# Handing the expert weights to the DMA queue one pair of rows later in a fused MoE, attention, MoE layer

## The chip, the cores and the metric

The kernel runs on one core of a Trainium2 chip. The metric is the device time of one execution in microseconds (us); a version is judged by the median of several executions.

## What is computed

The input `x` is 2048 tokens (4 sequences of 512) of 512 numbers in float32. The layer adds three terms to it, one after the other:

```
x = x + 0.5 * moe(layernorm(x))
x = x + attention(layernorm(x))        # 32 heads, causal, ALiBi, q and k layer-normed
x = x + 0.5 * moe(layernorm(x))        # same weights as the first

def moe(x):
    logits = x @ W_gate + b_gate                       # 8 experts
    top2   = the two experts with the largest logits
    y_all  = relu(x @ W_e[e] + b_e[e])                 # for each expert e, 512 x 512 weights
    return mean of the two chosen y_all
```

## The kernel before, in words

The program is a row of blocks: routing 1, experts 1, qkv, attention, routing 2, experts 2. The change lies in `route_block`, which is called for both routings.

**What a routing block does.** The 2048 tokens are taken as 8 *pairs* of row tiles; pair `u` holds tiles `2u` and `2u+1` of 128 tokens each. For each pair the block loads the rows (`load_x`), computes the layer norm on VectorE (DVE), ending in two `TENSOR_SCALAR` instructions that write `xn` (line 1289), stores the plain rows into the accumulator (`store_x`, line 1021) and the normalised rows into DRAM for the later gather (`store_xn`, line 1025). TensorE (PE) transposes the normalised rows (`transpose`, four matmuls per tile by line 1121), ScalarE (ACT) copies the transpose out of PSUM (`copy`, line 1209), and PE multiplies it with the gate weights (`gate`, line 1144). When the gates of all 16 tiles are there, DVE starts the choice of the experts at line 1298 (`route_logits`), a long chain which ends in the tables that the expert block reads.

**The expert weights.** Beside this the block brings the 8 MB of expert weights in, as 16 *pieces* of 512 KB, two per expert. Piece `n` is loaded into `w_lo` (`load_weights`, line 1031), ACT rounds it into `w_hi` (`weights(n)`, line 1213), and GpSimd (POOL) takes the difference back into `w_lo` (line 1109). No piece is used before the expert block.

**Routing 2 has more to do per pair.** There the attention's output projection is done on the way (`proj`): `load_o` brings in a tile of attention output (line 1017), PE transposes it (`o_transpose`), ACT splits it (`o_split`, line 1204), DVE takes the rest (`o_rest`, line 1251), PE multiplies (`out_proj`, twelve matmuls per tile, lines 144 to 146), and DVE adds the result to the row (`add_x`, line 1257) before its layer norm.

**What sets the order.** Every engine runs its own instruction list in the order in which it is written, and waits on semaphores. All the loads and stores named here are issued by SyncE (SP) from one list. ACT's list for pair `u` of routing 2 is: `o_split(2u+2)`, `weights(2u)`, `o_split(2u+3)`, `copy` of the two tiles of pair `u-1`, `weights(2u+1)`; in routing 1 it is the same without the `o_split`. DVE's list for pair `u` of routing 2 is: `add_x(2u)`, `o_rest(2u+2)`, statistics, `add_x(2u+1)`, `o_rest(2u+3)`, statistics, the reciprocal root, the two writes of `xn`. PE's list for pair `u` is: the gates of pair `u-2`, `out_proj(2u)`, `o_transpose(2u+2)`, `out_proj(2u+1)`, `o_transpose(2u+3)`, the transposes of pair `u-1`.

On SP, `store_xn(u)` waits until the `xn` of pair `u` is written, and all that is written behind it in SP's list waits with it. `load_x(u)` waits for its buffer from pair 4 on.

Of the kernel before, what the change touches and what calls it, by code (L numbers as in the profile page):

```python
# [900 lines left out]
def route_block(nc, prefix, ex, x_in, xn_dram, acc, w_gate, b_gate, w_e, b_e, o_dram=None, wo_turned=None, w_qkv=None, w_turned=None):  # L901
# [4 lines left out]
    with ExitStack() as ctx:  # L906
# [93 lines left out]
        PAIRS = TILES // 2  # L1000


        def pair_rows(dram, u):
            return dram[2 * P * u:2 * P * (u + 1), :].rearrange("(p k) d -> p k d", k=2)

        @block.sync
        def _(sp):
            def load_x(u):
                if u >= XR:
                    sp.wait_ge(xn_done, 2 * (u - XR) + 2)  # L1010
                    sp.wait_ge(x_stored[u % XR], 16 * (u // XR))
                sp.dma_start(x[u % XR][:, :, :], pair_rows(x_in, u)).then_inc(x_loaded[u % XR], 16)

            def load_o(t):
                if t >= 2:
                    sp.wait_ge(o_tr, t - 1)
                sp.dma_start(o[t % 2][:, :], pair_rows(o_dram, t // 2)[:, t % 2, :]).then_inc(o_loaded[t % 2], 16)

            def store_x(u):
                sp.wait_ge(sum_done if proj else x_loaded[u % XR], 2 * u + 2 if proj else 16 * (u // XR + 1))  # L1020
                sp.dma_start(pair_rows(acc, u), x[u % XR][:, :, :]).then_inc(x_stored[u % XR], 16)

            def store_xn(u):
                sp.wait_ge(xn_done, 2 * u + 2)
                sp.dma_start(pair_rows(xn_dram, u), xn[u % 2][:, :, :]).then_inc(xn_stored[u % 2], 16)

            def load_weights(n):

                if n >= WR:
                    sp.wait_ge(w_hi_done, n - WR + 1)  # L1030
                sp.dma_start(ex.w_lo[:, 2 * n:2 * n + 2, :].bitcast(F32), w_e[n // 2, :, :].rearrange("(p c) h -> p c h", c=C)
                             [:, 2 * (n % 2):2 * (n % 2) + 2, :]).then_inc(w_loaded[n % WR], 16)

            if proj:
                load_o(0)
                load_o(1)
            load_x(0)
            sp.dma_start(g_raw[:, :, :], w_gate.rearrange("(c p) e -> p c e", p=P)).then_inc(g_loaded, 16)
            sp.dma_start(bg_bc[:, :], b_gate.rearrange("(a e) -> a e", a=1).to_broadcast([P, E])).then_inc(bias_loaded, 16)
            if proj:  # L1040
                load_o(2)
                load_o(3)
            load_x(1)
            load_weights(0)
            load_weights(1)
            for u in range(PAIRS):
                if u + 2 < PAIRS:
                    load_x(u + 2)
                if u >= 1:
                    store_xn(u - 1)  # L1050
                if u + 1 < PAIRS:
                    load_weights(2 * u + 2)
                    load_weights(2 * u + 3)
                if proj and 2 * u + 4 < TILES:
                    load_o(2 * u + 4)
                    load_o(2 * u + 5)
                store_x(u)

            def load_wq(n):
                if n < 2:  # L1060

                    sp.wait_ge(xn_done, 2 * (n + XR) + 2)
                    sp.wait_ge(x_stored[n], 16 * (PAIRS // XR))
                else:
                    sp.wait_ge(wq_tr, 2 * n - 2)
                sp.dma_start(w_stage[n % 2][:, :, :], w_qkv[2 * P * n:2 * P * (n + 1), :].rearrange("(k p) d -> p k d", p=P)
                             ).then_inc(wq_loaded[n % 2], 16)

            if w_qkv is not None:
                load_wq(0)  # L1070
                load_wq(1)
            store_xn(PAIRS - 1)
            if w_qkv is not None:
                for n in range(2, WQ_PAIRS):
                    load_wq(n)
                sp.wait_ge(wq_tr, 2 * WQ_PAIRS)
            for i in range(XR):
                sp.wait_ge(x_stored[i], 16 * (PAIRS // XR))
            sp.wait_ge(xn_done, TILES)
            sp.dma_start(ex.bias[:, :], b_e.rearrange("(a e) h -> a (e h)", a=1).to_broadcast([P, E * D])).then_inc(ex.bias_loaded, 16)  # L1080
            sp.wait_ge(bias_loaded, 16)
            for par in range(2):
                sp.wait_ge(xn_stored[par], 16 * (PAIRS // 2))
# [488 lines left out]
```

## Time and profile before

| | |
|---|---|
| median of 3 executions | 1024.22 us (1021.04 to 1028.01) |
| the profiled execution | 1027.31 us, its span 1025.6 us |
| routing 1, from the start to the first expert gather | 92.8 us |
| routing 2, from the end of attention to the first expert gather | 747 to 873 us of the span |
| PE busy | 873.8 us, 85% of the span |
| DVE busy | 638.0 us, 62% |
| ACT busy | 444.2 us, 43% |
| POOL busy | 353.1 us, 34% |

Times in rows of the trace are counted from the start of the span. The profiled execution is 3.1 us above the median and within the range of the three. A bracket at the end of a row of the timeline gives the idle time of the engine before it, and what ended it.

### The profile page before, as it was taken

How to read it: one execution, taken by the hardware profiler on the slowest of the kernel's cores; microseconds unless marked ns; L12 is line 12 of the kernel's file. 1: busy time of each engine (PE TensorE's matmuls, PEld its weight loads, DVE VectorE, ACT ScalarE, POOL GpSimd, SP SyncE). 2: the span in 40 equal slices, each digit the busy share in tenths (PEclk: the TensorE clock that was granted, in tenths of full speed). 3: DMA queues.
4: the chain of work that ended last, by engine and by line, in shares of the span. 5: the costliest groups of instructions: out<-in, count | busy, mean ns of one | idle time of the engine just before them, and what ended most of it. 6: DMA issues, size and time to landing. Idle time of an engine off the chain costs nothing. (4 is left out here: it accounts for less than half of the span.)

```text
span 1025.6 us, 20208 instructions
## 1 busy us (share of the span) xinstructions
PE 873.8 (85%) x6688; PEld 646.5 (63%) x6689; DVE 638.0 (62%) x1296; ACT 444.2 (43%) x818; POOL 353.1 (34%) x342
## 2 busy tenths in 40 slices
PE   4874999992999989769999999999859993799994
PEld 4773888871777767645555555555447872688883
DVE  7955344433988877757777777777246768244441
ACT  3431333332244434527767677777623430233331
POOL 6723677763123222300000000000034420677764
PEclk9995999996999999959999999999979975799997
DMA  9954588762165599464666666562078850477863
GB/s 339 373 194 170 106 149 149 144 120 71 42 194 171 173 222 232 154 178 115 159 136 135 134 131 137 137 147 75 23 237 300 314 196 31 109 145 145 149 130 51
DMA packets 112859, 162.08 MB, mean 158 GB/s; under 512 B 16864, under 2 KB 74336, under 8 KB 112512
## 3 DMA queue, kind: packets, MB, share of 16 engines
q1 hardware_dynamic: 94928, 123.85, 41.5%
q0 software_dynamic: 17856, 37.25, 19.1%
q8 instruction: 45, 0.74, 0.3%
q14 instruction: 30, 0.25, 0.1%
HBM read 97.44 MB, written 67.37 MB: 161 GB/s over the span
## 5 line engine op out<-in xcount | busy, mean ns | idle before, releaser
L829 DVE TENSOR_REDUCE att_part<-att_s_ps 128x2 f32<-128x1024 f32 (+2 forms) x160 | 195.5, 1225 | 60.9 <-PE att_s_ps L677 60.5
L791 ACT ACTIVATE att_prob<-att_st_ps 128x512 f32<-128x512 f32 x320 | 173.7, 595 | 78.7 <-PE att_st_ps L703 78.6
L144 PE MATMUL exp_z_ps<-ex_w_hi,exp_xT_hi 128*128 x312 | 132.1, 423 | 1.3 <-DVE exp_xT_lo L1482 0.7
L146 PE MATMUL exp_z_ps<-ex_w_hi,exp_xT_lo 128*128 x312 | 126.2, 404 | 0.0
L145 PE MATMUL exp_z_ps<-ex_w_lo,exp_xT_hi 128*128 x312 | 125.8, 403 | 0.0
L1482 DVE TENSOR_TENSOR exp_xT_lo<-exp_t_ps,exp_xT_hi 128x512 fp32r<-128x512 f32 x78 | 54.0, 692 | 107.2 <-ACT exp_xT_hi L1468 107.2
L1475 ACT ACTIVATE exp_y<-exp_y 128x512 f32<-128x512 f32 x72 | 45.5, 632 | 168.7 <-DVE exp_y L1494 168.7
L1109 POOL TENSOR_TENSOR ex_w_lo<-ex_w_lo,ex_w_hi 128x1024 fp32r<-128x1024 f32 x32 | 76.2, 2395 | 96.2 <-ACT ex_w_hi L1213 64.9
L716 PE MATMUL att_pv_ps<-att_prob,att_v_sb 128*32 128x256 f32 (+2 forms) x1280 | 101.4, 391 | 1.8 <-ACT att_oT L796 1.8
L1410 POOL DMA_INDIRECT exp_xg<-xn,ex_token_of x78 | 78.1, 1002 | 66.2 <-SPq L1382 38.7
L641 POOL CAST att_m_parts<-att_part 128x28 fp32r<-128x28 f32 x32 | 6.6, 208 | 270.3 <-DVE att_part L833 270.3
L1494 DVE TENSOR_TENSOR exp_y<-exp_z_ps,ex_bias 128x512 f32<-128x512 f32 x72 | 49.8, 692 | 67.0 <-PE exp_z_ps L146 66.4
L144 PE MATMUL qkv_o_ps<-qkv_w_hi,qkv_xT_hi 128*128 128x512 f32 x192 | 81.8, 426 | 1.9 <-DVE qkv_xT_lo L436 1.6
L146 PE MATMUL qkv_o_ps<-qkv_w_hi,qkv_xT_lo 128*128 128x512 f32 x192 | 77.5, 404 | 0.0
L145 PE MATMUL qkv_o_ps<-qkv_w_lo,qkv_xT_hi 128*128 128x512 f32 x192 | 77.5, 403 | 0.0
L1434 POOL DMA_INDIRECT out<-exp_y,ex_row_of x39 | 62.1, 1591 | 27.4 <-DMA out<-exp_y,ex_row_of 12.3
L144 PEld LDWEIGHTS exp_z_ps<-ex_w_hi,exp_xT_hi 128*128 128x128 f32 x312 | 61.3, 197 | 14.2 <-issue 2.7
L1448 PE MATMUL exp_t_ps<-exp_ident,exp_xg 128*128 128x128 f32 x312 | 51.4, 290 | 21.3 <-DMA exp_xg<-xn,ex_token_of 21.3
L146 PEld LDWEIGHTS exp_z_ps<-ex_w_hi,exp_xT_lo 128*128 128x128 f32 x312 | 60.2, 193 | 14.2
L1448 PEld LDWEIGHTS exp_t_ps<-exp_ident,exp_xg 128*128 128x128 f32 x312 | 50.2, 206 | 29.6 <-issue 17.2
L145 PEld LDWEIGHTS exp_z_ps<-ex_w_lo,exp_xT_hi 128*128 128x128 f32 x312 | 60.4, 194 | 11.3
L656 PE MATMUL att_s_ps<-st_masks 64*128 64x256 bf16 (+1 forms) x640 | 57.7, 260 | 10.4 <-PEq L211 7.8
(199 smaller groups left out, 1644.0 us busy)
## 6 DMA issues: line engine op xcount, KB each, us to landing
ex_w_lo<-in_L_ffn_W_e SPq DMA_DIRECT2D x32, 512.0 KB, 5.7
v_vals<-st_vals SPq DMA_DIRECT2D x16, 512.0 KB, 2.8
q_parts<-st_partq SPq DMA_DIRECT2D x32, 256.0 KB, 3.4
k_parts<-st_partk SPq DMA_DIRECT2D x32, 256.0 KB, 3.7
att_v_sb<-v_vals SPq DMA_DIRECT2D x32, 256.0 KB, 3.7
ex_bias<-in_L_attn_hidden_states SPq DMA_DIRECT2D x8, 512.0 KB, 7.8
acc<-ex_bias SPq DMA_DIRECT2D x8, 512.0 KB, 8.6
xn<-route_xn SPq DMA_DIRECT2D x8, 512.0 KB, 5.5
```

What stands on the lines that cost most here:

```text
L144: nc.tensor.matmul(out, x_hi[:, s], w_hi(c), start=(c == 0), stop=False)
L145: nc.tensor.matmul(out, x_hi[:, s], w_lo(c), start=False, stop=False)
L146: last = nc.tensor.matmul(out, x_lo[:, s], w_hi(c), start=False, stop=(c == C - 1))
L656: nc.tensor.matmul(blocks_of(banks[half], where), mine[:, 0, :], rhs, start=(c == 0), stop=False, skip_group_check=True)
L716: last = nc.tensor.matmul(pv_ps[VW * h:VW * (h + 1), j * P + c0:j * P + c1], v_sb[n % RING][:, j, VW * h:VW * (h + 1)], prob[n % 2][:, col ...
L791: nc.scalar.activation(prob[n % 2][:, col:col + 512], st_ps[(e + half) % 3][:, :], ACT.Exp).then_inc(exp_done, 1)
L829: nc.vector.tensor_reduce(out, src, X_AXIS, ALU.max, negate=True).then_inc(red_done, 1)
L1109: nc.gpsimd.tensor_tensor(ex.w_lo[:, 2 * n:2 * n + 2, :], ex.w_lo[:, 2 * n:2 * n + 2, :].bitcast(F32), ex.w_hi[:, 2 * n:2 * n + 2, :].bitc ...
L1410: nc.gpsimd.indirect_dma_start(out=xg[s % RING][:, :], out_offset=None, in_=xn_dram[:, :], in_offset=bass.IndirectOffsetOnAxis(ap=ex.token ...
L1434: nc.gpsimd.indirect_dma_start(out=acc[:, :], out_offset=bass.IndirectOffsetOnAxis(ap=ex.row_of[:, s:s + 1], axis=0), in_=y[s % RING], in_ ...
L1448: last = nc.tensor.transpose(t_ps[r % 2][:, c * P:(c + 1) * P], xg[r][:, c:D:C], ident[:, :])
L1482: nc.vector.tensor_tensor(xT_lo[r % 2][:, :], t_ps[r % 2][:, :], xT_hi[r % 2][:, :].bitcast(F32), ALU.subtract).then_inc(lo_done, 1)
```

## The change

Before, pieces 0 and 1 are issued ahead of the loop, and the turn of pair `u` issues the pieces `2u+2` and `2u+3`. Now the turn of pair `u` issues the pieces `2u` and `2u+1`, from `u = 1` on. The turn of pair 0 issues none, and the turn of pair 7, which issued none before, issues pieces 14 and 15. Nothing is added or taken away: the same 16 transfers stand one turn later in SP's list.

```
                 if u >= 1:
                     store_xn(u - 1)
-                if u + 1 < PAIRS:
-                    load_weights(2 * u + 2)
-                    load_weights(2 * u + 3)
+                if u >= 1:
+
+                    load_weights(2 * u)
+                    load_weights(2 * u + 1)
                 if proj and 2 * u + 4 < TILES:
```

The lists of ACT, DVE, PE and POOL keep their order. SP's list of routing 2 from the load of pair 1's rows on, before (`ex_bias<-acc` is `load_x`, `ex_w_lo` a pair of pieces, `route_o` the attention output, `out` `store_x`, `xn` `store_xn`):

```order
L1012 DMA ex_bias<-acc 128x1024
L1031 DMA ex_w_lo<-in_L_ffn_W_e 128x1024 x2
L1012 DMA ex_bias<-acc 128x1024
L1031 DMA ex_w_lo<-in_L_ffn_W_e 128x1024 x2
L1017 DMA route_o<-o_vals 128x512 x2
L1021 DMA out<-ex_bias 128x1024
L1012 DMA ex_bias<-acc 128x1024
L1025 DMA xn<-wo_turned 128x1024
L1031 DMA ex_w_lo<-in_L_ffn_W_e 128x1024 x2
```

And the same place in the changed program:

```order
L1012 DMA ex_bias<-acc 128x1024
L1031 DMA ex_w_lo<-in_L_ffn_W_e 128x1024 x2
L1012 DMA ex_bias<-acc 128x1024
L1017 DMA route_o<-o_vals 128x512 x2
L1021 DMA out<-ex_bias 128x1024
L1012 DMA ex_bias<-acc 128x1024
L1025 DMA xn<-wo_turned 128x1024
L1031 DMA ex_w_lo<-in_L_ffn_W_e 128x1024 x2
```

The pair of pieces that stood ahead of pair 0's stores has gone; pieces 2 and 3 now stand behind the store of pair 0's `xn`, where 4 and 5 stood.

SP's list at the end of routing 1, before, from the store of pair 4's `xn` on (`acc<-ex_bias` is `store_x` here, `in_L_attn_Wqkv` the load of the attention weights):

```order
L1025 DMA xn<-route_xn 128x1024
L1031 DMA ex_w_lo<-in_L_ffn_W_e 128x1024 x2
L1021 DMA acc<-ex_bias 128x1024
L1025 DMA xn<-route_xn 128x1024
L1031 DMA ex_w_lo<-in_L_ffn_W_e 128x1024 x2
L1021 DMA acc<-ex_bias 128x1024
L1025 DMA xn<-route_xn 128x1024
L1021 DMA acc<-ex_bias 128x1024
L1066 DMA ex_bias<-in_L_attn_Wqkv 128x2x512 x2
```

And the changed program, from the same store on:

```order
L1025 DMA xn<-route_xn 128x1024
L1031 DMA ex_w_lo<-in_L_ffn_W_e 128x1024 x2
L1021 DMA acc<-ex_bias 128x1024
L1025 DMA xn<-route_xn 128x1024
L1031 DMA ex_w_lo<-in_L_ffn_W_e 128x1024 x2
L1021 DMA acc<-ex_bias 128x1024
L1025 DMA xn<-route_xn 128x1024
L1031 DMA ex_w_lo<-in_L_ffn_W_e 128x1024 x2
L1021 DMA acc<-ex_bias 128x1024
```

The last pair of pieces, 14 and 15, now stands behind the store of pair 6's `xn`; it stood behind that of pair 5.

## Rows read from the trace of the kernel before

**Rows 1.** Busy time by stretch: window, length, engines, PE clock, DMA share, GB/s
```profile
9.00:29.00 20.00, 14.05 (x61) 12.47 (x62) 18.69 (x45) 10.74 (x14) 16.03 (x7) 1.00 1.02 419
46.00:54.00 8.00, 6.52 (x29) 5.63 (x28) 7.45 (x20) 2.98 (x4) 5.11 (x3) 1.00 0.87 265
771.00:775.00 4.00, 4.00 (x12) 3.09 (x11) 1.29 (x2) 1.40 (x2) 2.38 (x1) 0.59 0.94 281
780.00:790.00 10.00, 9.70 (x59) 8.23 (x59) 7.59 (x23) 4.06 (x6) 5.14 (x3) 1.00 0.89 316
```
**Rows 2.** ACT's waits for the pieces, routing 1 (total us, times, longest)
```profile
ACT ex_w_hi L1213 <- DMA ex_w_lo<-in_L_ffn_W_e: 32.5, 9, 8.0
```
**Rows 3.** ACT's waits for the pieces, routing 2
```profile
ACT ex_w_hi L1213 <- DMA ex_w_lo<-in_L_ffn_W_e: 1.2, 1, 1.2
```
**Rows 4.** Timeline of SP, routing 2: start, us, queue, line, transfer
```profile
781.39 0.32 SPq L1025 DMA_DIRECT2D xn<-wo_turned  x1
...
791.40 0.65 SPq L1031 DMA_DIRECT2D ex_w_lo<-in_L_ffn_W_e  x1
```
**Rows 5.** DMA issues of 781.3 to 782: last figure us from issue to landing
```profile
xn<-wo_turned SPq DMA_DIRECT2D x1, 512.0 KB, 3.0
ex_w_lo<-in_L_ffn_W_e SPq DMA_DIRECT2D x1, 512.0 KB, 4.9
```
**Rows 6.** DMA issues of 791 to 791.6, the next pair's first piece
```profile
ex_w_lo<-in_L_ffn_W_e SPq DMA_DIRECT2D x1, 512.0 KB, 5.2
```
**Rows 7.** Timeline of ACT, routing 2, turn of pair 2
```profile
782.56 1.05 ACT L1213 ACTIVATE ex_w_hi<-ex_w_lo 128x1024 fp32r<-128x1024 f32 x1
785.28 0.60 ACT L1204 ACTIVATE route_oT_hi<-route_o_ps 128x512 fp32r<-128x512 f32 x1 [1.67 <-PE route_o_ps L1121]
785.77 1.08 ACT L1209 ACTIVATE route_xT<-route_t_ps 128x512 f32<-128x512 f32 x2
```
**Rows 8.** Timeline of DVE, routing 2
```profile
769.28 1.00 DVE L1289 TENSOR_SCALAR wo_turned<-ex_bias,route_mv,route_rstd 128x512 f32<-128x512 f32 x2
...
785.91 0.69 DVE L1251 TENSOR_TENSOR route_oT_lo<-route_o_ps,route_oT_hi 128x512 fp32r<-128x512 f32 x1 [0.30 <-ACT route_oT_hi L1204]
...
789.86 1.15 DVE L1289 TENSOR_SCALAR wo_turned<-ex_bias,route_mv,route_rstd 128x512 f32<-128x512 f32 x2
...
830.01 3.19 DVE L1289 TENSOR_SCALAR wo_turned<-ex_bias,route_mv,route_rstd 128x512 f32<-128x512 f32 x2
...
846.00 0.29 DVE L1298 TENSOR_TENSOR route_logits<-route_g_ps,route_bg_bc 128x128 f32<-128x128 f32 x1 [5.12 <-PE route_g_ps L1144]
```
**Rows 9.** Timeline of PE, routing 2
```profile
770.16 0.66 PE L1121 MATMUL route_o_ps<-route_ident,route_o 128*128 128x128 f32 x4 [2.72 <-DMA route_o<-o_vals]
...
786.41 1.95 PE L1144 MATMUL route_g_ps<-route_g_raw,route_xT 128*128 128x8 f32 x16 [0.30 <-ACT route_xT L1209]
...
840.48 1.97 PE L1121 MATMUL route_t_ps<-route_ident,wo_turned 128*128 128x128 f32 x8 [1.71 <-DVE wo_turned L1289]
842.28 3.59 PE L1144 MATMUL route_g_ps<-route_g_raw,route_xT 128*128 128x8 f32 x16
```
**Rows 10.** Timeline of ACT, routing 1: piece 14
```profile
54.97 1.06 ACT L1213 ACTIVATE ex_w_hi<-ex_w_lo 128x1024 fp32r<-128x1024 f32 x1 [5.34 <-DMA ex_w_lo<-in_L_ffn_W_e]
```
**Rows 11.** Timeline of PE, routing 1: gates of pair 6, transposes of pair 7
```profile
56.56 3.58 PE L1144 MATMUL route_g_ps<-route_g_raw,route_xT 128*128 128x8 f32 x16 [1.81 <-ACT route_xT L1209]
59.99 1.95 PE L1121 MATMUL route_t_ps<-route_ident,route_xn 128*128 128x128 f32 x8
```
**Rows 12.** Timeline of DVE, routing 1: `xn` of pair 7, start of the choice
```profile
57.17 2.02 DVE L1289 TENSOR_SCALAR route_xn<-ex_bias,route_mv,route_rstd 128x512 f32<-128x512 f32 x2
65.49 0.29 DVE L1298 TENSOR_TENSOR route_logits<-route_g_ps,route_bg_bc 128x128 f32<-128x128 f32 x1 [6.30 <-PE route_g_ps L1144]
```
**Rows 13.** Instructions of line 1289, routing 1: ns min/median/max
```profile
L1289 DVE TENSOR_SCALAR route_xn<-ex_bias,route_mv,route_rstd x16: 534/1394/2652, 8.5 to 58.7; 128x512 f32<-128x512 f32 x16
```
**Rows 14.** Instructions of line 1109, routing 1: ns min/median/max
```profile
L1109 POOL TENSOR_TENSOR ex_w_lo<-ex_w_lo,ex_w_hi x16: 2338/2358/2540, 11.3 to 71.1; 128x1024 fp32r<-128x1024 f32 x16
```

## The prediction

> **What bounds the kernel now.** The change touches only the two routing blocks, so I read those two stretches, first by busy time, then by waits, then instruction by instruction at the last pair. What is to be found is the thing that DVE's choice of experts waits for, since all that follows hangs on it.
>
> Routing 1 is bound by its transfers. From 9 to 29 us the DMA engines are full at 419 GB/s [rows 1], so one transfer of 512 KB (524,288 bytes) takes 1.25 us of the queue, and ACT waits nine times, 32.5 us in all, for a piece to land [rows 2]. These waits matter, because ACT's list puts `weights(2u)` ahead of the copies of pair u-1. The end shows it: piece 14 releases ACT at 54.97, the copies of pair 6 follow [rows 10], PE gates pair 6 from 56.56, released by them, and transposes pair 7 from 59.99 without a wait [rows 11]; its gates end the block, and the choice starts at 65.49 [rows 12]. From the landing of piece 14 to the choice there are 10.5 us of unbroken chain. A second path ends at the same point: the `xn` of pair 7 is written at 57.17 + 2.02 = 59.19 [rows 12].
>
> Routing 2 is bound by PE: 9.70 of 10 us busy at the full clock between 780 and 790 [rows 1], and ACT waits for a piece once, 1.2 us, in the whole block [rows 3]. The pieces are there ahead of their use, because they were issued a turn earlier. Piece 4, which ACT takes at 782.56 [rows 7], stood behind the store of pair 0's `xn`, written at 769.28 + 1.00 = 770.28 [rows 8], and so was issued some 12 us before its use.
>
> **The change, routing 2.** Call X(u) the time at which the `xn` of pair u is written. After the change, pieces 2u and 2u+1 are issued behind the store of X(u-1) and wanted by ACT within turn u. Behind `weights(2u)` in ACT's list stand `o_split(2u+3)` and the copies of pair u-1. DVE's `o_rest(2u+3)` waits for that split, and X(u) comes behind it in DVE's list. So a loop of one pair closes, which was two pairs long before: X(u-1), issue, landing, `weights`, `o_split`, `o_rest`, X(u). Its length from rows:
> - X to the issue of the first piece: the write of pair 2 ends at 789.86 + 1.15 = 791.01 [rows 8], the piece is issued at 791.40 [rows 4]: 0.39 us.
> - Issue to landing behind the `xn` store on a short queue: 4.9 and 5.2 us [rows 5, 6]; I take 5.05. The neighbours in SP's list are the same as before, so the queue in front should be too.
> - `weights(2u)` on ACT: 1.05 us [rows 7].
> - Start of the split to start of the rest: 785.91 - 785.28 = 0.63 us [rows 7, 8].
> - `o_rest` to X: 791.01 - 785.91 = 5.10 us [rows 8].
>
> That makes 12.2 us. Turns 1 to 6 have the split, so six of them lie between X(0), which the change does not move (770.28), and X(6): 770.3 + 73.3 = 843.6. Before, X(6) was 830.01 + 3.19 = 833.20 [rows 8], so this is 10.4 us later.
>
> What was late before is covered then: PE needs some 9.65 us per pair (X(2) at 791.01 against X(1), which released the store at 781.39 [rows 4]) and will wait some 2.5 us in each. The row loads and `route_o` loads that now go ahead of pieces 2 and 3 do arrive sooner, but nothing is won by it, because X(1) waits for piece 2.
>
> The tail: `weights(14)` stands ahead of the copies of pair 6, so after X(6) come 0.39 + 5.05 + 1.05, then 0.64 from the copies to the gates (785.77 to 786.41 [rows 7, 9]), the gates of pair 6, and from the transposes of pair 7 to the choice 846.00 - 840.48 = 5.52 [rows 8, 9]. The gates took 1.95 us at 786, in the stretch of full clock, and 3.59 at 842 [rows 1, 9]. PE will have waited there, so both are possible: 14.6 or 16.2 us, against 846.00 - 833.20 = 12.8 before. The middle is 2.6 more. Routing 2: **+13.0 us**.
>
> The least is set by the landing: a store behind an empty queue lands in 3.0 us [rows 5], plus one transfer of 1.25 us makes 4.25 and a loop of 11.4, so +8. The most: a piece behind a longer queue. In routing 1 the pace of five transfers per pair is 6.25 us; with that as the landing time the loop is 13.4 and the block +20.
>
> The Trainium skill bears on the landing. "DMA: Bandwidth & Descriptors", section "Rules for kernel authors", says to issue a DMA early and wait for it late, so that its fixed cost overlaps with compute; that rule speaks against this change. The same page, section "Anatomy of one DMA — SWDGE (gpsimd) path", fits some 2.0 us plus the bytes at 436 GB/s, for transfers that GpSimd issues; an estimate from it for a store and a piece of 512 KB is 4.4 us, a loop of 11.6 and a block of +9. The rows above show 4.9 and 5.2 on SP's queue, and I keep to them.
>
> **The change, routing 1.** No `o_split` stands here, but the copies still stand behind `weights(2u)`. In SP's list piece 14 had 34 transfers of 512 KB ahead of it (8 row loads, 6 `acc` and 6 `xn` stores, 14 pieces); now it has 36, one `acc` and one `xn` store more. On a full queue that is 2 x 1.25 = 2.5 us, and the chain of 10.5 us behind piece 14 carries it to the choice. It need not be all: between 46 and 54 the queue moved only 265 GB/s [rows 1], and where the queue has run empty, a store ahead of the piece costs less. Against it stands a gain on the other path: the last `xn` should come earlier, since its rows go ahead and fewer pieces lie on POOL in its way (below). But that path only ended level with the pieces' path, so its gain is not seen. I take **+2.0 us**, from -1 (the queue's slow stretch does not come again) to +4 (it comes, and the store of pair 6 is late).
>
> **The sum.** 13.0 + 2.0 = 15 us. The profiled execution, 1027.3 us with 1.7 us outside its span, would become 1042.3; the median of the three runs is 3.1 us below it, so I predict 1024.2 + 15 = **1039 us**. The experts, qkv and attention carry the shift without a change: no piece is wanted there before all are long done.
>
> **The rivals.**
> - *Rows first pays: faster.* In routing 1 the two `xn` writes take 0.53 us alone, but 1.39 in the median and up to 2.65 [rows 13], while POOL works on a piece for 2.36 us [rows 14]: 16 x (1.39 - 0.53) is some 14 us in which pieces hold up rows. Each pair then has its pieces behind it and not beside it. If the writes were the only path, the last pair would be ready about two piece times earlier, 4 to 5 us, and with routing 2 still fed in time the kernel would take 1020 us. It decides at ACT: for a choice 4 us earlier piece 14 must land by 51 us, where it landed at 55 with two transfers less ahead of it, and for routing 2 to keep its old mean of 62.9 / 6 = 10.5 us per pair a piece must land 3.3 us after its issue. The nine waits [rows 2] and the 4.9 us [rows 5] speak against it. The Trainium skill, "SBUF — State Buffer", section "SBUF: two separate sides", says that VectorE and GpSimd share a port pair as an exclusive lock for a whole instruction; by that rule such writes wait for the rest of a piece, and the kernel with the lock out of the way is this rival's 1020. The trace agrees with the lock (2.65 against 0.53 us). I give it 5%.
> - *The loop is looser than I count.* With the least landing, 4.25 us, routing 2 loses 8 us, and with the better end of routing 1 the sum is +7: 1031, within 1%. For it speaks that the queue in routing 2 is shorter when one pair's rows no longer share a turn with PE's full pace; against it, that the store and the two pieces were alone behind one row load in [rows 5, 6] already. 13%.
> - *PE falls to the low clock and becomes the bound.* Behind a wait of 2.72 us [rows 9] PE's granted clock was 0.59 of full from 771 to 775 [rows 1], so mostly the lower level, 1.2 GHz in place of 2.4. In the loop it waits 2.5 us per pair. A short fall fits into that wait. If the clock stays low for a whole pair, 9.65 us of PE work become 19.3, 7 us beyond the loop; in two of the six pairs that is +14: 1053. 10%.
>
> **How the numbers follow.** The forecast has 72%, the rivals 5, 13 and 10. Its own ends are +8 - 1 and +20 + 4; ends of both at once are unlikely, so I take it from 1030 to 1048, which holds the looser loop too; the faster rival, the PE rival and a few outliers lie outside, under 2 in 10. A measurement of this kernel tells about 1%, 10 us, from no change. Slower by more than that means above 1034.5: most of the forecast and all of the PE rival, 0.79. Within 1%: the looser loop, the rows-first case in part and the lowest of the forecast, 0.18. Faster: 0.03.
>
> **What would show it.** Right: in routing 2, ACT waits for pieces in turns 1 to 7 where it waited once, the writes of `xn` stand 12.2 us apart, each piece is issued 0.4 us behind a write, PE is idle some 2 us per pair, and the choice starts near 859. In routing 1 the copies of pair 6 still stand right behind a wait for piece 14, and the choice starts at 66 to 68. Wrong: the writes of `xn` stay about 10 us apart, or PE waits for nothing in routing 2; or routing 1 ends by more than 2 us earlier.

## The result, and the profile after

The changed kernel takes **1046.87 us** (median of 4 executions, 1044.92 to 1052.87) against 1026.12 us for the kernel before (4 executions, the three shown above and one more beside it). The ratio is 1.0202, with a 95% interval of 1.0164 to 1.024: 17 to 25 us slower. The forecast was +15 us and 1039 us, in a range of 1030 to 1048: right in direction, and in range near its upper end, but 5 to 6 us too small. The profiled execution took 1046.21 us, its span 1044.5 us, 18.9 us more than the span before. The lines from 1052 on stand one number higher than before; each later version is quoted by the line numbers of its own kernel.

In **routing 2** ACT now waits for pieces, and PE for ACT. The waits of the two engines, 745 to 865 us (total us, times, longest):

```profile
ACT ex_w_hi L1214 <- DMA ex_w_lo<-in_L_ffn_W_e: 30.2, 7, 10.2
...
PE route_g_ps L1145 <- ACT route_xT L1210: 17.3, 7, 6.3
```

Before, ACT waited once, 1.2 us [rows 3], and PE's waits at the same place were short:

```profile
PE route_g_ps L1144 <- ACT route_xT L1209: 2.1, 7, 0.3
```

The loop can be read off one turn, that of pair 4. SP's timeline:

```profile
810.31 0.32 SPq L1025 DMA_DIRECT2D xn<-wo_turned  x1
810.67 1.27 SPq L1031 DMA_DIRECT2D ex_w_lo<-in_L_ffn_W_e  x2
...
822.58 0.32 SPq L1025 DMA_DIRECT2D xn<-wo_turned  x1
```

Its first piece in the DMA issues of 810.5 to 811 (last figure, us from issue to landing):

```profile
ex_w_lo<-in_L_ffn_W_e SPq DMA_DIRECT2D x1, 512.0 KB, 5.2
```

ACT's timeline of the same turn:

```profile
810.99 0.60 ACT L1205 ACTIVATE route_oT_hi<-route_o_ps 128x512 fp32r<-128x512 f32 x1 [3.92 <-PE route_o_ps L1122]
815.91 1.06 ACT L1214 ACTIVATE ex_w_hi<-ex_w_lo 128x1024 fp32r<-128x1024 f32 x1 [4.31 <-DMA ex_w_lo<-in_L_ffn_W_e]
816.87 0.58 ACT L1205 ACTIVATE route_oT_hi<-route_o_ps 128x512 fp32r<-128x512 f32 x1
```

And DVE's:

```profile
809.13 1.15 DVE L1290 TENSOR_SCALAR wo_turned<-ex_bias,route_mv,route_rstd 128x512 f32<-128x512 f32 x2
...
817.48 0.69 DVE L1252 TENSOR_TENSOR route_oT_lo<-route_o_ps,route_oT_hi 128x512 fp32r<-128x512 f32 x1 [2.95 <-ACT route_oT_hi L1205]
...
821.43 1.12 DVE L1290 TENSOR_SCALAR wo_turned<-ex_bias,route_mv,route_rstd 128x512 f32<-128x512 f32 x2
```

The write of `xn` ends at 810.28, the piece is issued at 810.67 and rounded from 815.91, the split follows at 816.87, the rest at 817.48, and the next write ends at 822.55: 12.27 us around, where the forecast had 12.2. ACT stood 4.31 us in front of the piece, with the split that DVE wanted behind it.

Not every turn is that clean. In the turn of pair 2 the split was released by PE and not by the piece, as ACT's timeline shows, and the stretch 783 to 788 by busy time (columns as in [rows 1]) shows why:

```profile
789.27 1.05 ACT L1214 ACTIVATE ex_w_hi<-ex_w_lo 128x1024 fp32r<-128x1024 f32 x1
791.99 0.60 ACT L1205 ACTIVATE route_oT_hi<-route_o_ps 128x512 fp32r<-128x512 f32 x1 [1.67 <-PE route_o_ps L1122]
```
```profile
783.00:788.00 5.00, 5.00 (x14) 3.78 (x13) 0.58 (x2) 0.00 (x0) 0.00 (x0) 0.50 0.68 199
```

PE had waited 6.3 us in the turn before and came back at the low level of its clock (granted 0.50, 1.2 GHz). It started 14 matmuls in those 5 us and was late for the split, which began 1.67 us behind the rounding that it would otherwise have followed at once. That turn took 14.1 us.

The tail, on DVE and on PE (two timelines):

```profile
846.21 1.15 DVE L1290 TENSOR_SCALAR wo_turned<-ex_bias,route_mv,route_rstd 128x512 f32<-128x512 f32 x2
...
864.92 0.29 DVE L1299 TENSOR_TENSOR route_logits<-route_g_ps,route_bg_bc 128x128 f32<-128x128 f32 x1 [9.43 <-PE route_g_ps L1145]
```
```profile
855.99 3.58 PE L1145 MATMUL route_g_ps<-route_g_raw,route_xT 128*128 128x8 f32 x16 [4.81 <-ACT route_xT L1210]
859.42 1.95 PE L1122 MATMUL route_t_ps<-route_ident,wo_turned 128*128 128x128 f32 x8
```

X(6) is 847.36, and the choice starts 17.6 us later (12.8 before [rows 8]). Piece 14 took 6.6 us to land (DMA issues of 847.6 to 848), and the gates of pair 6 took the slow 3.58 us, at a granted clock of 0.50 from 856.00 to 859.40:

```profile
ex_w_lo<-in_L_ffn_W_e SPq DMA_DIRECT2D x1, 512.0 KB, 6.6
```

The choice had been forecast near 859. From its first transfer (747.07 before, 748.17 now) to the choice, routing 2 takes 116.8 us in place of 98.9: **+17.8 us**.

In **routing 1** the chain behind piece 14 is the same, later. ACT, PE and DVE:

```profile
57.75 1.06 ACT L1214 ACTIVATE ex_w_hi<-ex_w_lo 128x1024 fp32r<-128x1024 f32 x1 [4.15 <-DMA ex_w_lo<-in_L_ffn_W_e]
```
```profile
59.35 3.58 PE L1145 MATMUL route_g_ps<-route_g_raw,route_xT 128*128 128x8 f32 x16 [1.74 <-ACT route_xT L1210]
62.78 1.95 PE L1122 MATMUL route_t_ps<-route_ident,route_xn 128*128 128x128 f32 x8
```
```profile
53.78 3.12 DVE L1290 TENSOR_SCALAR route_xn<-ex_bias,route_mv,route_rstd 128x512 f32<-128x512 f32 x2
...
68.28 0.29 DVE L1299 TENSOR_TENSOR route_logits<-route_g_ps,route_bg_bc 128x128 f32<-128x128 f32 x1 [11.39 <-PE route_g_ps L1145]
```

Piece 14 lands 2.8 us later than before [rows 10], and the choice starts 2.8 us later [rows 12], a little behind the 66 to 68 of the forecast. The rows did go ahead: the last `xn` is written at 56.90 in place of 59.19. But PE takes it up at 62.78 only, so that gain buys nothing. The shift of 2.8 us does not reach routing 2 whole: in this pair of traces the first gather of experts 1 comes 2.4 us later (92.81 and 95.16), and routing 2 starts 1.1 us later.

### The profile page after: what moved, and what is told of

Its sections match the earlier page's. It is cut to its first block and busy times, and to the rows that moved or that the text cites. A ratio compares the mean times of both kernels' runs of the same rounds, so it can differ in the third digit from the quotient of the medians.

```text
span 1044.5 us, 20208 instructions
## 1 busy us (share of the span) xinstructions
PE 874.2 (84%) x6688; PEld 648.2 (62%) x6689; DVE 632.9 (61%) x1296; ACT 444.1 (43%) x818; POOL 352.1 (34%) x342
## 5 line engine op out<-in xcount | busy, mean ns | idle before, releaser
L1145 PE MATMUL route_g_ps<-route_g_raw,route_xT 128*128 128x8 f32 x256 | 49.7, 331 | 33.4 <-ACT route_xT L1210 33.4
L1145 PEld LDWEIGHTS route_g_ps<-route_g_raw,route_xT 128*128 128x128 f32 x256 | 48.2, 289 | 38.3 <-ACT route_xT L1210 38.3
L1435 POOL DMA_INDIRECT out<-exp_y,ex_row_of x39 | 62.1, 1591 | 27.4 <-issue 12.2
L1449 PEld LDWEIGHTS exp_t_ps<-exp_ident,exp_xg 128*128 128x128 f32 x312 | 50.4, 206 | 30.8 <-issue 17.6
```

Source lines behind the costliest of these rows:

```text
L1145: last = nc.tensor.matmul(g_ps[:, t * E:(t + 1) * E], xT[t % 2][:, c * P:(c + 1) * P], g_raw[:, c, :], start=(c == 0), stop=(c == C - 1))
L1435: nc.gpsimd.indirect_dma_start(out=acc[:, :], out_offset=bass.IndirectOffsetOnAxis(ap=ex.row_of[:, s:s + 1], axis=0), in_=y[s % RING], in_ ...
L1449: last = nc.tensor.transpose(t_ps[r % 2][:, c * P:(c + 1) * P], xg[r][:, c:D:C], ident[:, :])
```

## The experiments

The theory is the loop: a piece issued behind the store of pair u-1, rounded by ACT in turn u ahead of what DVE needs for pair u. Its rivals: the pieces cost by their place in the queue or on POOL beside the writes of `xn` (queue and port), or by what PE's clock does after a wait. Each ratio is against the kernel before on the same chip, which took 1028.05, 1024.06 or 1026.06 us there. The us given with a ratio are worked out from it; the difference of the two medians deviates from them by up to 1.3 us.

**One block at a time.** In `route_block`, the new condition for one of the two blocks and the old one for the other (in the second run with `if proj`):

```
-                if u + 1 < PAIRS:
-                    load_weights(2 * u + 2)
-                    load_weights(2 * u + 3)
+                if not proj:
+                    if u >= 1:
+                        load_weights(2 * u)
+                        load_weights(2 * u + 1)
+                elif u + 1 < PAIRS:
+                    load_weights(2 * u + 2)
+                    load_weights(2 * u + 3)
```

Routing 1 alone. 

> Pieces later in routing 1 alone. Loop theory (a piece wanted by ACT in the turn in which it is issued; its price in routing 1 is two transfers in front of piece 14, since ACT copies pair 6 behind it): choice of experts of routing 1 starts 2 to 3 us later (67.5 to 68.5), the whole +2 to +3 us, 1028 to 1029. Rows-first rival: 3 to 4 us faster. If the blocks did not add up (a shift of routing 1 being lost in qkv and attention): 0 to +1.

Measured: 1031.76 against 1028.05 us, ratio 1.0036 (1.0010 to 1.0062): +3.7 us, slightly more than expected. The choice of this trace stands at 71.16 us, later than in the whole change (68.28) with the same code up to there, so single traces of this block differ by some 3 us. Without the change in routing 1 it stands at 65.49, 64.64 and 64.02 in three traces (the kernel before, routing 2 alone, the half dose below), so both traces with the change are later than all three.

Routing 2 alone. 

> Pieces later in routing 2 alone. Loop theory: X(0) unmoved, then some 12.5 us between the writes of xn, +17 to +18 us in the block, 1043 us in all, ACT waiting some 30 us for pieces. Clock theory gives the same sum here. Rows-first rival: not above 1030.

Measured: 1047.6 against 1028.05 us, ratio 1.0178 (1.0126 to 1.0229): +18.3 us, as the loop theory expected. ACT waits 29.0 us for pieces, and routing 2 takes 113.8 us to its choice. The two parts add up to the whole within their intervals.

**The loop cut at ACT.** In the changed program:

```
                 if proj and u + 1 < PAIRS:
                     o_split(2 * u + 2)
-                if u < PAIRS:
-                    weights(2 * u)
-                if proj and u + 1 < PAIRS:
                     o_split(2 * u + 3)
                 if u >= 1:
                     copy(2 * u - 2)
                     copy(2 * u - 1)
+                if u < PAIRS:
+                    weights(2 * u)
                 if u < PAIRS - 1:
                     weights(2 * u + 1)
```

> The changed program with one thing moved: in ACT's list each turn's two roundings of pieces stand behind that turn's splits and copies; the DMA order is that of the changed kernel. Loop theory: the loop over one pair is cut, the writes of xn in routing 2 stand about 10 us apart again and its choice comes within 2 us of the kernel before; in routing 1 the copies no longer wait for piece 14 and the choice comes at 61 to 65; in all 1020 to 1026. Queue theory (late pieces cost because they share the queue with rows and stores, or lie beside them on the port): nothing in the DMA order has changed, so still 1040 or more. Clock theory: PE waits less, so it too recovers, but only as far as PE's waits go.

Measured: 1030.3 against 1028.05 us, ratio 1.0013 (0.9989 to 1.0036). The same DMA order now costs nothing that can be told, so the queue theory falls. The gain below the kernel before that was expected (1020 to 1026) did not come. The trace shows it missing in routing 1, where the choice starts at 65.56, no earlier than before. With the roundings last in the turn, piece 14 no longer stands ahead of the copies of pair 6, but it stands ahead of those of pair 7, as ACT and PE show:

```profile
60.24 1.06 ACT L1214 ACTIVATE ex_w_hi<-ex_w_lo 128x1024 fp32r<-128x1024 f32 x1 [5.20 <-DMA ex_w_lo<-in_L_ffn_W_e]
61.21 1.06 ACT L1210 ACTIVATE route_xT<-route_t_ps 128x512 f32<-128x512 f32 x2
```
```profile
61.84 3.58 PE L1145 MATMUL route_g_ps<-route_g_raw,route_xT 128*128 128x8 f32 x16 [1.84 <-ACT route_xT L1210]
```

In routing 2 the pieces have moved onto the writes of `xn`. The 16 writes take 19.9 us where they took 11.5; DVE's timeline has two of them at 4.65 us together:

```profile
801.13 4.65 DVE L1289 TENSOR_SCALAR wo_turned<-ex_bias,route_mv,route_rstd 128x512 f32<-128x512 f32 x2
```

The block does not visibly pay for it: from its first transfer to its choice it takes 96.9 us in this trace, against 98.9 before and 116.8 in the changed kernel.

**The loop cut at SP.** In the changed program, the pieces of a turn go ahead of the wait for `xn`:

```
                 if u >= 1:
-                    store_xn(u - 1)
-                if u >= 1:
-
                     load_weights(2 * u)
                     load_weights(2 * u + 1)
+                    store_xn(u - 1)
```

> The changed program with one thing moved: in SP's list the two pieces of a turn stand ahead of that turn's store of xn, so that they are issued without the wait for it; still a turn later than before, and ACT's list is that of before. Loop theory: in routing 2 the issue comes about 5 us earlier in the loop, a piece lands near X and is wanted 6 us later, so the loop is slack and the block is within 3 us of the kernel before; routing 1 about +1 us; in all 1026 to 1031. If lateness by a turn is itself the cost (not the wait in front): 1040 or more.

Measured: 1034.3 against 1028.05 us, ratio 1.0063 (1.0034 to 1.0092): +6.5 us, two thirds of the cost gone, but at the upper end of what was expected (1026 to 1031, with a kernel before of 1024). ACT still waits for pieces six times in routing 2, 14.5 us in all. So a piece that is a turn later is still wanted before it lands in most turns, even without the wait in front.

**ACT's list alone, on the kernel before.** The edit at ACT with the DMA order of before. 

> The kernel before, with its DMA order, and in ACT's list each turn's two roundings behind the splits and copies. Tells whether the place in ACT's list is free where pieces are early. Loop theory: in routing 1 the copies no longer wait for piece 14, but the xn of pair 7 (59.2) then sets the end, choice 1 us earlier at most; routing 2 unchanged, as ACT waited there only once; in all -2 to +1 us. Port rival (a piece on POOL beside the writes of xn holds them up): the pieces move closer to those writes, as in the run with ACT's list changed, where the writes of routing 2 took 19.9 us in place of 11.5; then +2 to +5 us.

Measured: 1028.93 against 1024.06 us, ratio 1.0047 (1.0022 to 1.0071): +4.8 us, in the port rival's range, but not in the block that it had pointed to. In routing 2 the writes of `xn` take 23.2 us in place of 11.5, and the block still takes 99.3 us, against 98.9. In routing 1 they take 28.5 us in place of 23.4, DVE goes from one pair to the next without a wait, and the last `xn` is written at 64.19 in place of 59.19. PE waits for it, and the choice moves from 65.49 to 69.31. So the edit is no gain by itself; it is only good against late pieces.

**Both cuts at once.** Pieces ahead of the store, rounded last in the turn. 

> Both cuts at once in the changed program: pieces issued ahead of the turn's store of xn, and rounded last in ACT's turn. Loop theory: no loop through a piece is left, so PE sets the pace in routing 2 and the transfers in routing 1; 1020 to 1028. Port rival: the writes of xn in routing 2 still take near 20 us and some turns are 12 us long, 1028 to 1032.

Measured: **1018.82** against 1024.06 us, ratio 0.9954 (0.9934 to 0.9974). This version beats both kernels, by 4.7 us over the kernel before. The port rival had expected 1028 or more, since the writes of `xn` in routing 2 would still be held up. They are (22.3 us), and the block takes 96.0 us all the same. Its choice in routing 1, on DVE:

```profile
61.33 0.29 DVE L1296 TENSOR_TENSOR route_logits<-route_g_ps,route_bg_bc 128x128 f32<-128x128 f32 x1 [4.52 <-PE route_g_ps L1143]
```

This is 4.2 us ahead of [rows 12]. Piece 14 is rounded at 53.05 in this trace, well before the copies of the last pair. These wait for PE, and PE for the last `xn`, written at 56.81. So the path through the rows, which the prediction called the second one, now sets the end of the block.

**The port taken out.** On the kernel before:

```
-    nc.gpsimd.tensor_tensor(ex.w_lo[:, 2 * n:2 * n + 2, :], ...
+    nc.gpsimd.tensor_tensor(ex.w_lo[0:1, 2 * n:2 * n + 1, 0:1], ...
```

The lines are shortened; the two operands are cut in the same way.

> The kernel before with the work of POOL on the pieces cut to one number each (the differences of the weights are left out, so the expert blocks multiply with wrong rests). The writes of xn are alone on the port: 16 x 0.53 = 8.5 us in routing 1 in place of 23. Rows-first rival (these writes set the end of routing 1): choice 6 to 9 us earlier, and as much in all, more with routing 2. Loop theory: piece 14 and the copies behind it set the end as well, so the choice is at most 3 us earlier; in all -4 to 0.

Measured: 1020.22 against 1024.06 us, ratio 0.9962 (0.9945 to 0.9980). The writes of `xn` in routing 1 (ns min/median/max), and its choice:

```profile
L1289 DVE TENSOR_SCALAR route_xn<-ex_bias,route_mv,route_rstd x16: 541/544/548, 8.5 to 49.6; 128x512 f32<-128x512 f32 x16
```
```profile
61.08 0.29 DVE L1298 TENSOR_TENSOR route_logits<-route_g_ps,route_bg_bc 128x128 f32<-128x128 f32 x1 [10.90 <-PE route_g_ps L1144]
```

With POOL out of the way every write takes 0.54 us, against 0.53 to 2.65 [rows 13]: what held them up was POOL's work. This agrees with the exclusive lock on the port pair shared by VectorE and GpSimd that the Trainium skill describes, "SBUF — State Buffer", section "SBUF: two separate sides". But 9 us less at the last write (50.2 us) gave only 4 at the choice, and PE shows why:

```profile
46.91 3.58 PE L1144 MATMUL route_g_ps<-route_g_raw,route_xT 128*128 128x8 f32 x16 [0.86 <-ACT route_xT L1209]
...
52.13 3.58 PE L1144 MATMUL route_g_ps<-route_g_raw,route_xT 128*128 128x8 f32 x16
```

The gates of pair 5 still start behind copies that stood behind a piece, number 12, for which ACT waited 3.27 us. From there on PE works without a gap to the choice. So PE ends the block here, and the gates of pair 6 no longer wait for piece 14 and its copies. The choice came 4.4 us earlier, where the loop theory had allowed 3.

The same edit on the changed kernel. 

> The changed kernel with POOL's work on the pieces cut to one number each (the differences of the weights are left out, as in the run on the kernel before). Loop theory: the loop through ACT has no POOL in it, so the writes of xn in routing 2 stand 12.2 us apart as with POOL's work, and against the kernel before without that work (0.996 of the kernel before) the change costs the same 18 to 20 us: +14 to +16 us over the kernel before. Port rival (late pieces cost because they lie beside the writes of xn): without them the change costs nothing, -4 to 0 us.

Measured: 1042.93 against 1026.06 us, ratio 1.0174 (1.0134 to 1.0215). Against the run just told, 1.0174 / 0.9962 = 1.021: without POOL's work the change costs as much as with it, some 22 us (18 to 20 expected). The port theory of the change's cost falls.

**Half the dose.** Later in routing 2 from turn 4 on:

```
-                if u + 1 < PAIRS:
+                if proj and u >= 3:
+                    if u >= 4:
+                        load_weights(2 * u)
+                        load_weights(2 * u + 1)
+                elif u + 1 < PAIRS:
```

> Pieces later in routing 2 alone, and there only from turn 4 on (turns 0 to 2 as before, turn 3 issues none). Loop theory: the writes of xn stand 9.6 us apart up to pair 3 and 12.2 to 12.6 for pairs 4, 5 and 6, and the tail behind pair 6 is that of the full dose: 3 x 2.8 + 2.7, so +10 to +12 us. If the cost were paid once, at the first turn whose pieces come late (PE's long wait and the low clock behind it): as much as the full dose, +17, or, if it were paid at the end alone, +3.

Measured: 1031.87 against 1024.06 us, ratio 1.0077 (1.0052 to 1.0102): +7.9 us. The writes of pairs 2 to 6:

```profile
786.18 1.12 DVE L1293 TENSOR_SCALAR wo_turned<-ex_bias,route_mv,route_rstd 128x512 f32<-128x512 f32 x2
797.39 1.15 DVE L1293 TENSOR_SCALAR wo_turned<-ex_bias,route_mv,route_rstd 128x512 f32<-128x512 f32 x2
809.49 1.13 DVE L1293 TENSOR_SCALAR wo_turned<-ex_bias,route_mv,route_rstd 128x512 f32<-128x512 f32 x2
821.57 1.15 DVE L1293 TENSOR_SCALAR wo_turned<-ex_bias,route_mv,route_rstd 128x512 f32<-128x512 f32 x2
833.74 1.12 DVE L1293 TENSOR_SCALAR wo_turned<-ex_bias,route_mv,route_rstd 128x512 f32<-128x512 f32 x2
```

The cost is paid turn by turn: once the pieces are late the ends of the writes stand 12.1, 12.1 and 12.1 us apart. A cost paid once, behind PE's long wait and low clock, would have been +17, and one paid at the end alone +3, so both fall. The sum was expected 2 to 4 us larger, because it took 9.6 us for a turn without the loop, where six turns of the kernel before take 62.9 us, 10.5 each: 3 x 1.6 and some 3 us of tail are the 8 measured.

**The faster version taken apart.** Both cuts in routing 1 alone. 

> The faster version taken apart: pieces ahead of the store of xn and last in ACT's turn in routing 1 alone, routing 2 as in the kernel before. If the gain of that version lies in routing 1 (its choice at 61.3 us against 65.5, nearly all pieces' waits of ACT off the copies): -4 to -5 us, the same as with both. If it lies in routing 2: -1 to +1.

Measured: 1023.92 against 1026.06 us, ratio 0.9968 (0.9943 to 0.9993), its choice of routing 1 at 61.2 us: -3.3 us, a little less than the -4 to -5 expected. By these values most of the gain lies there; whether routing 2 adds to it the two intervals do not tell.

## Why the prediction was right, and where it fell short

- *The loop of one pair in routing 2.* Right, and shown: it vanishes when ACT's list is changed, with the DMA order left as it is, and its turn takes 12.1 us in the half dose, for 12.2 forecast. In the changed kernel X(0) to X(6) took 76.1 us, in routing 2 alone 74.8, without POOL's work 73.3; the forecast was 73.3. Of the excess of 2.8 us of the first, 1.9 lie in the turn of 14.1 us behind PE's low clock. The rival on PE's clock was true to that extent: one turn late by 2 us, not a new bound. In the other two runs waits of 5.3 and 5.6 us at the same place were followed by turns of 12.6 and 12.7 us.
- *The tail*, forecast at 14.6 to 16.2 us behind X(6): 17.6 in the changed kernel, 15.6 in routing 2 alone. The gates did run at the low clock (granted 0.50), and piece 14 took 6.6 us where 5.05 had been put in; with routing 2 alone it took 5.1, and no run tells why. The first pieces of the other turns landed in 4.9 to 5.5 us, as the rows of before had said. The estimate of 4.4 us from the Trainium skill, "DMA: Bandwidth & Descriptors", section "Anatomy of one DMA — SWDGE (gpsimd) path", was further off.
- *The term that was mis-sized* is thus routing 2, +13.0 us forecast and +17.8 in the trace: 2.8 us in the loop, 2.1 in the tail. The forecast's ends, +8 and +20, let the landing time stretch the loop but not the tail; with it in both they come out at +7 and +21, and the measured block lies inside. One trace of before also stood for a block that varies: with routing 2 untouched, the run of routing 1 alone needed 95.1 us to its choice, where [rows 8] come from 98.9. With both cuts in routing 1 alone it took 98.9 again.
- *Routing 1*, +2.0 forecast for two transfers in front of piece 14: 2.8 in the trace, 1.0 to 6.4 by the interval of that part alone. The claim that an earlier last `xn` buys nothing held. The claim that the blocks in between carry the shift without a change did not hold to the microsecond: 1.1 of the 2.8 us were left at the start of routing 2.
- *Rows first pays.* The held-up writes are real: without POOL's work on the pieces the kernel before gains 4 us. But this change does not collect that. The gain with both cuts is another one, since the writes are still held up there (two of 3.41 us together at the last pair of routing 1); most of it lies in routing 1, where the copies of the last pair no longer stand behind piece 14.

What stays open: in routing 1 the same code brought piece 14 in at 57.75 in one trace and at 60.6 in another. I did not find what slows the queue there, and no run was aimed at it.

## What to carry to other kernels

Before a prefetch is moved later, look whether something that the next issue waits for stands behind its use. Follow the ring through the lists: what the DMA queue waits for, who uses the data, what stands behind that use in its engine's list, and whether this comes back to the queue's wait. Where a loop closes, its time per turn is the whole chain with the landing time in it, and it decides as soon as it is longer than the bound engine's turn (12.2 us against 9.65 here). Two cuts were tried here. The use put last in its turn took the cost away, the issue put ahead of the wait two thirds of it, and only both together were faster than the kernel before.

## What the runs showed that was not expected

Moving ACT's roundings to the end of the turn, which looked free, made the kernel before 0.5% slower. It puts POOL's pieces of 2.4 us beside the writes of `xn` in both blocks, but only routing 1 visibly pays, where the last `xn` then sets the end. In routing 2 the writes grew by 8 to 12 us in three versions, and the block took 96.0 to 99.3 us, where three traces without an edit in it have 95.1 to 98.9.

One wait of 6.3 us on PE had a cost behind it: the next out-projection ran at a granted clock of 0.50, and the following turn took 14.1 us where a clean one took 12.3.

The granted clock does not tell PE's rate everywhere. In routing 1 the 16 gate matmuls of a pair take 3.58 us [rows 11] at a granted clock of 1.00 (read from 56.50 to 60.00 us in the kernel before); in routing 2 they take 1.95 at 1.00 and 3.58 at 0.50. No run here shows why.
